# Building the sparse matrix of a graph kernel: table words fetched four and thirteen at a time

## The reference

```python
def _L0_gnn_ref(...):   # h[src] and |h[dst]-h[src]|, summed over dst, then dense
def _L1_gnn_ref(...):   # two attention layers over the edges
def _L2_gnn_ref(features, src, dst, weight, bias):
    h = features * jax.lax.rsqrt(deg_out)[:, None]
    agg = jax.ops.segment_sum(h[src], dst, num_segments=n)
    out = (agg * jax.lax.rsqrt(deg_in)[:, None]) @ weight + bias
    return jax.nn.relu(out)
def _gcn_conv(x, src, dst, W, b, n):          # twice in layer 3
    out = jax.ops.segment_sum(norm[:, None] * (x @ W)[src], dst, num_segments=n)
    return out + b
```

## Time and profile before

| what | value |
|---|---|
| median of 3 runs | 8588.86 us (8587.01 to 8589.87) |
| the profiled execution | 8586.1 us |
| its span, first to last instruction | 8584.3 us |
| TensorE busy over the span | 6531.4 us (76%) |
| matrix build, first L933 to last L935 | 5879.4 to 6898.4 us |
| granted TensorE clock in the matrix build | 0.50 |

### The profile page before, as it was taken

The page is one execution under the profiler, slowest core; times in us unless marked ns, Lnnn a source line. Parts: engine busy times, 40 slices in busy tenths (PEclk is TensorE's granted clock), DMA queues, the critical chain, the costliest instruction groups (busy, mean ns, idle before and its releaser), DMA issues. The chain is left out here.

```text
span 8584.3 us, 131134 instructions
## 1 busy us (share of the span) xinstructions
PE 6531.4 (76%) x32021; PEld 4285.8 (50%) x32022; DVE 4752.3 (55%) x13173; ACT 1981.8 (23%) x3928; POOL 2418.5 (28%) x2515
## 2 busy tenths in 40 slices
PE   7997998577765456666656666666777799999999
PEld 3443444566665456666546666653333344444433
DVE  8999888555553477777556777656666611100000
ACT  2552554122221111111321111132333300000000
POOL 0000000477773037777206777700000000000000
PEclk9999999799997678888778888775555589999999
DMA  1000000111112023333203333402444477777777
GB/s 30 0 0 0 0 0 4 42 51 51 51 51 21 4 77 105 105 105 105 40 24 102 104 104 105 101 7 99 166 167 165 165 265 290 273 287 286 278 284 270
DMA packets 313131, 941.63 MB, mean 110 GB/s; under 512 B 80180, under 2 KB 130634, under 8 KB 280776
## 3 DMA queue, kind: packets, MB, share of 16 engines
q1 hardware_dynamic: 204360, 666.67, 21.1%
q0 software_dynamic: 106496, 272.79, 12.3%
q10 hardware_dynamic: 2176, 0.85, 0.0%
HBM read 752.56 MB, written 186.24 MB: 109 GB/s over the span
## 5 line engine op out<-in xcount | busy, mean ns | idle before, releaser
L588 POOL DMA_INDIRECT ACC<-tab_kv,STAGE x1664 | 1589.2, 955 | 1333.2 <-DMA STAGE<-IDX 827.0
L588 POOL DMA_INDIRECT SCR<-tab_h,STAGE x832 | 822.4, 988 | 1837.5 <-DMA STAGE<-IDX 1584.3
L664 PE MATMUL PS<-Q 128*128 128x416 f16 x6464 | 1175.0, 340 | 93.5 <-DVE Q L1368 93.5
L746 PE MATMUL PS<-SCR 128*128 128x137 f32 x3328 | 636.7, 346 | 736.6 <-DVE ACC L1476 692.0
L954 PE MATMUL PS<-ACC,Q 128*128 128x512 f32 (+3 forms) x2548 | 1052.0, 570 | 13.8 <-DMA ACC<-adj 13.8
L746 PEld LDWEIGHTS PS<-SCR 128*128 128x128 f32 x3328 | 531.9, 234 | 823.0 <-DVE ACC L1476 775.5
L664 PEld LDWEIGHTS PS<-Q 128*128 128x128 f16 x6464 | 611.6, 98 | 656.9 <-issue 198.2
L1476 DVE TENSOR_TENSOR ACC<-ACC,PS 128x137 f32 (+1 forms) x2496 | 835.6, 335 | 177.5 <-PE PS L750 51.6
L1090 ACT ACTIVATE SCR<-PS 128x512 f32<-128x512 f32 x624 | 372.6, 597 | 2296.9 <-PE PS L717 2296.9
L728 PE MATMUL PS<-Q,SCR 128*128 x4992 | 795.0, 312 | 0.0
L1366 DVE TENSOR_SCALAR Q<-Y,ACC 128x832 f16<-128x832 f16 x1616 | 697.8, 432 | 124.5 <-PE PS L664 124.2
(11 more groups left out here) (281 smaller groups left out, 7383.7 us busy)
## 6 DMA issues: line engine op xcount, KB each, us to landing
ACC<-adj SPq DMA_DIRECT2D x252, 1792.0 KB, 6.7
adj<-ACC SPq DMA_DIRECT2D x637, 256.0 KB, 2.0
ACC<-tab_kv,STAGE POOLq DMA_INDIRECT x1664
SCR<-tab_h,STAGE POOLq DMA_INDIRECT x832
tab_kv<-SCR SPq DMA_DIRECT2D x14, 896.0 KB, 4.1
ACC<-adj SPq DMA_DIRECT2D x21, 448.0 KB, 3.7
tab_h<-SCR SPq DMA_DIRECT2D x7, 448.0 KB, 3.0
out_x<-X SPq DMA_DIRECT2D x12, 256.0 KB
```

Source lines behind the costliest of these rows:

```text
L588: nc.gpsimd.indirect_dma_start(G[:, q, j, 0:w], None, table, bass.IndirectOffsetOnAxis(STAGE[:, u, q * S4 + j:q * S4 + j + 1], 0))\
L664: ins = nc.tensor.matmul(SUMS[:, at:at + w], OHP[:, u, k, :], OHS[:, u, q * w:(q + 1) * w], start=first and u == 0, stop=last and u == RIN ...
L746: ins = nc.tensor.matmul(dst, oh, M[:, u % 2, j, :], start=True, stop=True)
```

## The change

TensorE loads the four words of a loop turn with one instruction at the start of the turn, and checks all four there; the waits for `emptied` and `built` stay in front of each word's items, and change places with each other. ScalarE loads the thirteen entries of a source tile with one instruction at the start of the tile, and checks all thirteen there.

```diff
-            def items(it, u):
-
-                i = it * 4 + u
-                pe.wait_ge(ad["built"], i + 1)
-                word = counts(pe, WORDS[:, bass.ds(i, 1)], COUNT, (CLASSES + 1) * COUNT - 1)[0]
-                pe.wait_ge(ad["emptied"], word >> 12)
-                for k in range(4):
...
+            def items(it, n):
+
+                words = counts(pe, WORDS[:, bass.ds(it * 4, n)], COUNT, (CLASSES + 1) * COUNT - 1)
+                for u, word in enumerate(words):
+                    pe.wait_ge(ad["emptied"], word >> 12)
+                    pe.wait_ge(ad["built"], it * 4 + (u + 1))
+                    for k in range(4):
...
             with pe.Fori(0, ITEMS // 16) as it:
-                for u in range(4):
-                    items(it, u)
-            for u in range(ITEMS // 4 % 4):
-                items(ITEMS // 16, u)
+                items(it, 4)
+            items(ITEMS // 16, ITEMS // 4 % 4)
...
                 j = it * 4 + u
+                ends = counts(act, CLASSN[:, bass.ds(j * NW, NW)], 1, ITEMS)
                 for g in range(NW):
-                    if g % 4 == 0:
-                        n = min(4, NW - g)
-                        ends = counts(act, CLASSN[:, bass.ds(j * NW + g, n)], 1, ITEMS)
-                    act.wait_ge(ad["items"], ends[g % 4])
+                    act.wait_ge(ad["items"], ends[g])
```

More of the change, by code:

```diff
@@ L921, in _ @@
                     .then_inc(ad["picked"], 1)
-            def items(it, u):
-                i = it * 4 + u
-                pe.wait_ge(ad["built"], i + 1)
-                word = counts(pe, WORDS[:, bass.ds(i, 1)], COUNT, (CLASSES + 1) * COUNT - 1)[0]
-                pe.wait_ge(ad["emptied"], word >> 12)
-                for k in range(4):
[L930 to L936, removed]
+            def items(it, n):
[4 more added lines that the diff above has]
+                    for k in range(4):
+                        unit = 8 ** k
+                        clear = PS[:, :].rearrange("p (n w) -> p n w", w=W4 // unit)[:, bass.ds(word & (7 * unit), 1), 0:1]
+                        bank = PS[:, 2048:4096].rearrange("p (n w) -> p n w", w=W4 // unit)[:, bass.ds(word & (3 * unit), unit), :]
+                        nc.tensor.matmul(clear.rearrange("p n w -> p (n w)"), OHS4[:, u % 2, k, :], ZEROC, start=True, stop=True,
+                                         skip_group_check=True)
+                        nc.tensor.matmul(bank.rearrange("p n w -> p (n w)"), OHS4[:, u % 2, k, :], OHD[:, u % 2, k, :],
+                                         start=False, stop=True, skip_group_check=True).then_inc(ad["items"], 1)
```

## The result

| | before | changed |
|---|---|---|
| median, 7 runs each | 8588.86 us (8582.5 to 8589.87) | 8615.77 us (8612.2 to 8625.17) |
| ratio | | 1.0037, 95% interval 1.0027 to 1.0047 |
| span of the profiled execution | 8584.3 us | 8614.1 us |
| first to last weight load of L933 | 5879.4 to 6898.3, 1018.9 us | 5875.4 to 6927.8, 1052.4 us |

The change makes the kernel 27 us slower. The forecast was 8599, with 8520 to 8655 as its range: the likeliest case has the side right (10 us over before), the size is short by 17 us. The loss lies in the matrix build, which is 33.5 us longer; the phases ahead end 4 us sooner.

What follows compares the result with a forecast made beforehand. TensorE's own instruction stream was taken as the bound of the matrix build. Its saving, late one-hots and the stall behind ScalarE's block gave -131 + 23 + 118 = +10 us, or 8599 against the median 8588.9; range 8520 to 8655.

Steps and rivals of the forecast that it cites:

- the likeliest case: ScalarE's load of thirteen: word by word in unaligned tiles, 16-byte pieces in aligned ones; 8599 us, chance 0.35.
- Part 1: TensorE's instruction stream in the build: fewer loads and waiting instructions save 1.48 us a turn, 131 us over 88.75 turns.
- Part 2: VectorE's one-hots in the build: with words closer together they come late once a turn, costing 23 us (6 to 30).
- Part 3: ScalarE's tile start: load and thirteen checks ahead of the first copy make TensorE stand in 48 tiles, 118 us.
- L: Length of ScalarE's load of thirteen: 3.2 us in 36 unaligned tiles, 1.1 in 13 aligned ones, mean 2.6.
- the three about L: ScalarE's load of thirteen: forecast 8599 (0.35); word by word always 8625 (0.20); pieces wherever they fit 8543 (0.32).
- The clock's case: TensorE granted 2.4 GHz in part of the build: some 27 us off any case, about 8572; chance 0.05.
- the two cases with cheap loads: ScalarE's load of thirteen: pieces wherever they fit, 8543 us, chance 0.32; one burst, 8511 us, chance 0.08.

Runs made afterwards that it cites:

- the first experiment: Only TensorE's half of the change, ScalarE loading 4, 4, 4 and 1 entries as before, against the kernel before: -75.8 us, ratio 0.992.
- words unaligned: Only TensorE's half of the change, its word table moved by one entry so loads start 4 bytes off, against the kernel before: +4.6 us, ratio 1.0005.
- the run with the mask: TensorE's half, ScalarE's loads of four aligned, TensorE's word checks replaced by a mask, against the kernel before: -166.7 us, again -171.4.
- the aligned table: Whole change, with 16 table entries a tile instead of 13 so ScalarE's loads start at 16 bytes, against the kernel before: -36.7 us, ratio 0.9961.
- eight words a turn: TensorE's half, ScalarE's fours aligned, mask for checks, loop turns of eight words instead of four, against the kernel before: -202.5 us, ratio 0.9789.

## Why the prediction held, and where it was off

- *TensorE's own stream is the bound, and nobody makes it wait.* Right: with ScalarE as before, the build gets shorter by what the instructions and the two waits leave (the first experiment), and another dear instruction once a turn (words unaligned) comes out at the end in full.
- *Part 1, 131 us.* Too high by some 16: the build is 33.5 us longer with 148.2 us more of waits (128.1 + 23.5, less 3.4 that stood in it before), so TensorE's own stream got 115 us shorter. The load of four has the median of L408, but its mean is 0.434, not 0.36: +7 us over 89 loads. Another 7 us are in the items, which follow each other inside a word 0.005 us later on average than before (0.4575 for 0.4525), 1420 times; why is not known. The last 2 are the four checks in a row: on TensorE they cost 0.288 us each in place of 0.293, where the sum took 0.04 us a turn for them. The bound given for the load alone was 18.
- *Part 2, 23 us for the one-hots.* Measured 23.5. The mechanism held (the run with the mask bears on it too), but part of the hit is luck: the prediction's own product, 0.3 x 88, is 26 and not 23, and for matmuls that end sooner it gave less, down to 6. In the changed kernel they did in part: 444 of the 1420 matmuls of L935 took 0.39 us in place of 0.59.
- *Part 3, a stall of L - 0.2 us in 48 tiles, with L = 3.2 and 1.1.* Mechanism and place held, and so did the price for each us: where the aligned table made L 2.22 us shorter, the stall fell by 2.15. The size of L was low: 3.53 and 1.33, mean 2.95 for 2.64. The working took 0.24 us for each further word, between the 0.2 of the cheapest unaligned load and the 0.33 of the dearest; the loads of thirteen ran at 0.27, which is what the mean of the loads of four, 1.10, would have given: (1.10 - 0.28) / 3. The waits are 128.1 for 118, but the 10 us do not lie where L was furthest off. The 36 unaligned tiles wait 2.99 us each, as forecast with the lower L (3.2 - 0.2); with the measured L it would be 3.3, so two errors cancel there. The 12 aligned tiles wait 1.73 us each where the forecast has 0.9. In these ScalarE first ends a turn of its loop of four tiles, so that the load starts 0.36 us after the start of the last copy in place of 0.07. The prediction left this loop end out. With the longer L it makes some 0.5 of the 0.8 us; the rest stays open.
- The sum with the measured terms: -131 + 16 + 23.5 + 128.1 - 3.4 = +33, against 33.5 for the build. So the forecast's error is +16 in part 1, +10 in part 3, +0.5 in part 2 and -3.4 for waits that stood in the kernel before already: 23 us more than its +10. The phases ahead took 4 us less, and the medians are 3 us closer to each other than the profiled executions, which leaves the 17.
- *The cases.* Of the three about L the aligned and unaligned loads decide for the forecast's: word by word where the start is unaligned, pieces of 16 bytes where it is aligned, and no change from one to the other inside a load, or the unaligned ones would have stayed near 2 us. The clock's case, which I gave 0.05, came true in part (0.69). It can't have given back much in the items: inside a word they follow each other after 0.457 us where the matmul took 0.39 us and after 0.458 where it took 0.59, so the pace is the sequencer's at either level. What it gave at the waits is not known.
- The chances had 0.26 for slower and 0.48 for faster. So the chances leaned to the wrong side; the likeliest case alone had it right. The side rested on a length that no row showed; the case chosen by the nearest row was the right one, but it was given less (0.35) than the two cases with cheap loads together (0.40). The rows had no sign of a load that changes from single words to pieces.
- *The rule of 200 ns for each register* of the Trainium skill ("Runtime: NRT & Kernel Launch", Instruction fetch mechanics) is given there for loads from HBM that the runtime puts in; these come from SBUF. It lies below the unaligned loads (0.27 us a word here) and far above the aligned ones: 0.334 us for four, 1.33 for thirteen.

## What to carry to other kernels

When work of a sequencer (loads, checks) is gathered to save its start-up, it also becomes one block: compare the block's length with how far the others may run ahead (here four banks: 3.9 us by the prediction's working, 4.0 by the mean stall, 2.95 + 3.75 - 2.67), and not with how idle the engine is. The same thirteen checks cost 86 us by the medians (100 by the build) in one piece, behind a load of 3.5 us, and next to nothing when each stood ahead of its own wait. And lay out tables so that a register load of several words starts at a multiple of 16 bytes; four bytes of displacement took back a gain of some 80 us.

## What was not expected of the hardware

- A register load of four unaligned words takes 1.38 us on average on TensorE's sequencer (up to 2.37) and 1.25 to 1.29 on ScalarE's in the same run; aligned it is 0.46 on TensorE (its part alone) and 0.41 on ScalarE. In the kernel before ScalarE's unaligned mean was 1.10. Loads of the two engines that meet are no account of this: beside a load of TensorE's sequencer ran 79 of the 108 in the kernel before and only 25 with TensorE's part alone, where the mean is 1.27.
- What goes with the price is VectorE's work at the time. In the kernel before, ScalarE's unaligned loads of four take 0.93 us on average (29 of them) while VectorE is idle for nine tenths of the load or more, and 1.27 (31) while it is busy for nine tenths or more; with TensorE's part alone 0.91 (13) and 1.33 (54). Aligned loads of thirteen take 1.01 (6) and 1.44 (26) in the run with the aligned table. In the kernel before VectorE is busy for 55% of such an unaligned load on average, with TensorE's part alone for 82%, which goes the way of the means. No edit has tried it, so it is not shown as the cause; TensorE's own loads can't be compared in this way, since in a kernel nearly all of them meet VectorE in one state.
- The prices of aligned loads fit pieces of four words: one word 0.28 to 0.30 us, four 0.31 to 0.33, eight 0.59, thirteen 1.00, each at its least.
- The granted clock in the build rose from 0.50 to 0.69 (changed), 0.74 (TensorE's part alone) and 0.87 (eight words a turn), and stayed at 0.50 with ScalarE's part alone. It rose in every run that loads the words of a turn together, even where TensorE waits longer than before (151.6 us in the changed kernel, 3.4 before). The windows of TensorE's part alone and of ScalarE's part alone:

```profile
6850.00:7700.00 850.00, 622.19 (x2571) 262.96 (x2568) 560.04 (x1604) 337.32 (x586) 0.00 (x0) 0.74 0.48 180
```

```profile
6850.00:7700.00 850.00, 579.46 (x2153) 233.23 (x2152) 469.66 (x1345) 281.98 (x491) 0.00 (x0) 0.50 0.40 151
```

- The other chips took 9500 to 9537 us for the kernel that takes 8589 on the first. The changed kernel shows where: its build starts at 6785.3 in place of 5875.4 us, and from there to the end it takes 2741.1 and 2738.7 us.
